# The message stage of a graph kernel: the last message product and the carry copies behind the third matrix product, and two pairs of PSUM banks that swap roles

## The reference

```
xs = concat(x[src, :8], x[dst, :8]); xv = the 3-vectors of both, 8 each
h  = sqrt(2) * relu(emb @ W1 / sqrt(10))                 # 16 hidden values per edge
w  = (h @ W2 / 4).reshape(E, 7, 16, 8)                   # seven weight blocks per edge
s_out, g_out = sums over xs, xv.y1 with w                # 8 and 8 values
v_out        = sums over xs*y1, xv, xv*y2 with w         # 8 vectors
out = concat(1.593*tanh(s_out), 1.593*tanh(g_out)[:, None] * v_out) * weight
layer = segment_sum(out, dst)
```

## Time and profile before

| what | value |
|---|---|
| median of 3 runs | 4437.76 us (4434.99 to 4440.44) |
| profiled execution: its own time | 4443.45 us |
| profiled execution: span from first to last instruction | 4441.7 us |
| DVE busy | 3024.5 us (68% of the span) |
| PE busy | 3333.9 us (75%) |
| POOL busy | 3235.5 us (73%) |
| ACT busy | 2187.2 us (49%) |
| mean granted TensorE clock | 0.953 |

### The profile page before, as it was taken

How to read it: one execution, slowest core, us unless ns; L and a number is a source line. 1 busy time by engine, 2 the same in 40 slices (tenths; PEclk the granted TensorE clock), 3 DMA queues, 4 the chain that set the end, 5 groups by cost and what they waited for, 6 DMA issues and landing times. The chain is left out here.

```text
span 4441.7 us, 66461 instructions
## 1 busy us (share of the span) xinstructions
PE 3333.9 (75%) x20487; PEld 2105.1 (47%) x20487; DVE 3024.5 (68%) x4871; ACT 2187.2 (49%) x4787; POOL 3235.5 (73%) x3260
## 2 busy tenths in 40 slices
PE   0005888888888888888888604999999999999940
PEld 0002333333333333323323203999999999999940
DVE  5525999999999999999999733344444544444432
ACT  3004555555555555555555311466666666666620
POOL 5777777777777777777774077777777777777756
PEclk9999999999999999999999856999999999999975
DMA  9311222222222222222222102133333333333311
GB/s 325 90 49 34 49 48 48 55 50 47 48 48 48 48 50 53 48 47 48 48 47 43 34 12 68 42 72 73 72 73 72 73 72 73 72 73 72 73 29 27
DMA packets 269592, 272.69 MB, mean 61 GB/s; under 512 B 182593, under 2 KB 237673, under 8 KB 266803
## 3 DMA queue, kind: packets, MB, share of 16 engines
q1 hardware_dynamic: 164150, 207.75, 17.0%
q0 software_dynamic: 104928, 60.74, 9.6%
q10 hardware_dynamic: 462, 3.60, 0.3%
HBM read 181.82 MB, written 90.02 MB: 61 GB/s over the span
## 5 line engine op out<-in xcount | busy, mean ns | idle before, releaser
L640 POOL DMA_INDIRECT edge<-xp_d,idx x1440 | 1447.3, 1005 | 439.1 <-issue 425.1
L900 DVE TENSOR_TENSOR prod<-G_ps,hid 128x1000 f32<-128x1000 f32 x1200 | 1400.4, 1195 | 125.8 <-PE G_ps L782 113.1
L1297 POOL DMA_INDIRECT x1e<-tab_d,idxb x1122 | 1105.4, 985 | 342.7 <-issue 336.4
L782 PE MATMUL G_ps<-FT,wst 32*128 32x500 f32 x4800 | 896.3, 633 | 356.8 <-DVE prod L900 350.0
L1346 PE MATMUL G_ps<-tb,hot 128*126 128x442 f32 (+1 forms) x3968 | 799.1, 358 | 0.9 <-DVE x1e L1371 0.8
L1346 PEld LDWEIGHTS G_ps<-tb,hot 128*126 128x126 f32 x3968 | 742.7, 187 | 38.4 <-DVE x1e L1371 2.0
L782 PEld LDWEIGHTS G_ps<-FT,wst 32*128 32x128 f32 x4800 | 246.3, 184 | 792.2 <-DVE prod L900 724.6
L811 PE MATMUL R_ps<-prod,red 128*32 128x500 f32 x4800 | 589.7, 594 | 0.0
L702 ACT ACTIVATE hid<-T_ps 128x500 f32<-128x500 f32 x400 | 233.8, 585 | 677.4 <-PE T_ps L802 677.1
L1346 PE MATMUL T_ps<-tb,hot 128*126 128x442 f32 x2000 | 416.4, 360 | 186.3 <-DVE one_d L1430 186.3
L1346 PEld LDWEIGHTS T_ps<-tb,hot 128*126 128x126 f32 x2000 | 376.6, 188 | 205.0 <-issue 186.4
(11 more groups left out here) (240 smaller groups left out, 4290.1 us busy)
## 6 DMA issues: line engine op xcount, KB each, us to landing
xd_d<-zeros SPq DMA_DIRECT2D x16, 1562.5 KB, 29.2
y_d<-ng SPq DMA_DIRECT2D x40, 595.0 KB
edge<-xp_d,idx POOLq DMA_INDIRECT x1440
xv<-xd_d SPq DMA_DIRECT2D x40, 560.0 KB
y_d<-zr SPq DMA_DIRECT2D x40, 560.0 KB
x1e<-tab_d,idxb POOLq DMA_INDIRECT x1122
edge<-sel_d SPq DMA_DIRECT2D x20, 750.0 KB
edge<-sel_d SPq DMA_DIRECT2D x20, 687.5 KB
```

The costliest lines, as they stand in the source:

```text
L640: nc.gpsimd.indirect_dma_start(out=edge_c[:, i, 8:8 + DIM], out_offset=None, in_=xp_d, in_offset=bass.IndirectOffsetOnAxis(col, 0)).then_i ...
L782: return Tn.matmul(G_ps[pair][:, a * 512:a * 512 + GW], wst[rows, r * 128:(r + 1) * 128], FT[k][rows, :], start=True, stop=True)
L900: V.tensor_tensor(prod[b][i][:, :].rearrange("p (a e) -> p a e", a=2), gv, hid[k][:, :].rearrange("p (a e) -> p a e", a=1).broadcast_to([1 ...
L1297: nc.gpsimd.indirect_dma_start(out=gx[b][:, c * T1:(c + 1) * T1], out_offset=None, in_=tab_d, in_offset=bass.IndirectOffsetOnAxis(idx[b][: ...
```

## The change

In the code of the message stage:

- `round1` is split. `round1a` (two products) is issued at the end of the group before, behind its `sum_round`s, and waits only for that group's first two products (`b_mul` >= 3n - 1). `round1b` (the other two) stands at the old place and waits for `b_mul` >= 3n as before. `b_G` is counted after each half.
- The bank pairs take turns: group n's first and third product read `G_ps[k]`, the second reads `G_ps[1 - k]`.
- On VectorE the second product has a wait of its own, for `round1b`.
- `post(2)` moves from between the second and third product of an odd group to the end of the even group before it, behind `post(0)`, `post(1)` and the scan.
- `carry_x` moves from gc 0 to the end of gc 9 of the chunk before; `carry_sums` moves, within gc 4, behind `post(1)`.

```diff
-                    def round1(n, k):
+                    def round1a(n, k):
                         pe.wait_ge(S("b_FT"), n + 1)
                         if some(n):
+                            pe.wait_ge(S("b_mul"), n * 3 - 1)
+                        product(k, 0, 0, k, 0)
+                        product(k, 0, 1, k, 1).then_inc(S("b_G"), 1)
+
+                    def round1b(n, k):
+                        if some(n):
                             pe.wait_ge(S("b_mul"), n * 3)
-                        product(k, 0, 0, 0, 0)
-                        product(k, 0, 1, 0, 1)
-                        product(k, 0, 2, 1, 1)
-                        product(k, 0, 3, 1, 0).then_inc(S("b_G"), 1)
+                        product(k, 0, 2, 1 - k, 1)
+                        product(k, 0, 3, 1 - k, 0).then_inc(S("b_G"), 1)
 
                     def round2(n, k):
                         pe.wait_ge(S("b_mul"), n * 3 + 1)
-                        product(k, 1, 0, 0, 0)
-                        product(k, 1, 1, 0, 1).then_inc(S("b_G2"), 1)
+                        product(k, 1, 0, k, 0)
+                        product(k, 1, 1, k, 1).then_inc(S("b_G2"), 1)
...
-                            round1(n, k)
+                            round1b(n, k)
...
+                            if not (last and g == G2 - 1):
+                                round1a(n + 1, 1 - k)
...
                         if i == 0:
                             dve.wait_ge(S("b_hid"), n + 1)
-                            dve.wait_ge(S("b_G"), n + 1)
+                            dve.wait_ge(S("b_G"), n * 2 + 1)
+                        if i == 1:
+                            dve.wait_ge(S("b_G"), n * 2 + 2)
...
-                        gv = G_ps[(0, 1, 0)[i]][:, :].rearrange("p (a e) -> p a e", a=2)[:, :, 0:GW]
+                        gv = G_ps[(k, 1 - k, k)[i]][:, :].rearrange("p (a e) -> p a e", a=2)[:, :, 0:GW]
...
-                            if k == 1 and not (first and g < 5):
-                                q = (g - 5) // 2
-                                post(2, t * RING + q, q % RING // PC, q % RING % PC, t if q >= 0 else t - 1)
-                            if gc == 0 and not (last and h == 1):
-                                carry_x(ch + 1, 1 - h)
-                            if gc == 4 and not (first and h == 0):
-                                carry_sums(ch - 1, 1 - h, t - 1 + h)
                             multiply(n, k, b, 2)
...
+                                if gc == GC - 1 and not last:
+                                    carry_x(ch + 2, h)
+                            else:
                                 q = (g - 4) // 2
+                                due = not (first and g < 4)
+                                if due:
+                                    for i in range(2):
+                                        post(i, t * RING + q, q % RING // PC, q % RING % PC, t if q >= 0 else t - 1)
+                                if scan:
+                                    scan()
+                                if gc == 4 and not (first and h == 0):
+                                    carry_sums(ch - 1, 1 - h, t - 1 + h)
+                                if due:
+                                    post(2, t * RING + q, q % RING // PC, q % RING % PC, t if q >= 0 else t - 1)
```

More of the change, by code:

```diff
@@ L845, in _ @@
                     transposes(1, 1, 0)
+                    round1a(0, 0)
                     turn(0, first=True)
@@ L974, in turn @@
                                     along(t * RING + q, q % RING)
-                            elif not (first and g < 4):
+                                if gc == GC - 1 and not last:
+                                    carry_x(ch + 2, h)
+                            else:
                                 q = (g - 4) // 2
[L977 to L980, removed]
+                                due = not (first and g < 4)
[8 more added lines that the diff above has]
+                                    post(2, t * RING + q, q % RING // PC, q % RING % PC, t if q >= 0 else t - 1)
                     for h in range(2):
@@ L993, in _ @@
                         along(p, p)
+                    carry_x(1, 1)
                     turn(0, first=True)
```

## The result

| what | before | after |
|---|---|---|
| median of 4 runs | 4439.10 us (4434.99 to 4441.09) | 4387.38 us (4385.00 to 4395.44) |
| ratio, 95% interval | | 0.9886 (0.9870 to 0.9901) |
| profiled execution: time, span | 4443.45, 4441.7 us | 4395.44, 4393.7 us |
| message stage, start of the first to start of the last product | 2150.1 us | 2099.4 us |
| one chunk, mean of 32 in the middle | 53.72 us | 52.57 us |

In the two traces, whose spans lie 48.0 us apart, the message stage is 50.8 us shorter, so the gain lies there and nowhere else. Medians and ratios are those of undisturbed executions; one of e6's four, which took 5387.23 us at a granted clock of 0.668, is left out.

What follows compares the result with a forecast made beforehand. VectorE's own order of work was taken to bound the message stage. Even groups, odd groups and gc 9 sum to 0.95 us per chunk, 38 us over 40 chunks; forecast median 4400 us, range 4389 to 4424.

Steps and rivals of the forecast that it cites:

- Odd groups: Groups losing `post(2)`: third product then held by `round2` alone, interval 5.37 to 5.22 us, 0.15 won each.
- gc 9: Chunk's last group into the next: first product no longer behind the third through `round1`, 0.30 us won a chunk.
- Even groups: Groups gaining `post(2)` behind the scan: it replaces the wait for TensorE, interval 5.43 to 5.42 us, 0.01 won each.
- the 0.14: Even groups: time in us from TensorE's end to the first product's start, kept unchanged in the new sum.
- Both chains stand at 5.41: Even groups: VectorE's and TensorE's new chains equally long at 5.41 us, so every delay shows.
- Stage ends: Both ends of the message stage: untouched by the change, no gain counted there.
- A: TensorE, odd groups: split halves run one after the other, +6 us, 4444, no change; chance 0.08.
- B: TensorE: halves in turn and each split costs its entry as well, slower at 4474 us; chance 0.06.
- C: Even groups: scan and `post(2)` pay full length and a gap, 30 us back, 4430, half of it 4415; chance 0.08.
- D: POOL: scans stretch gathers until they bind, 22 us come back, 4422; chance 0.06.
- The estimate was 54: POOL: room in us between last gather's end and last `turned` after the change, 91 before it.
- estimate of 10.48 a piece: POOL: a piece's eight gathers at 1.31 us each take 10.48 us, undisturbed 10.0; not binding.

Runs made afterwards that it cites:

- e6: The kernel after, with `turned` moved between second and third product in odd groups other than gc 9; 4355.99 us, ratio 0.9817.
- e3: The kernel before, with VectorE's order of the kernel after (`post(2)` and carry copies moved), `round1` whole; 4410.72 us, ratio 0.9935.
- e8: e3 with VectorE's two waits ahead of the first product swapped; 4394.21 us, ratio 0.9902.
- e1: The kernel before, with only VectorE's two waits ahead of the first product swapped; 4416.16 us, ratio 0.9952.
- e2: The kernel after, with VectorE's order of the kernel before (`post(2)` and carry copies back), `round1` still split; 4401.18 us, ratio 0.9917.
- e4: The kernel after, but the first product of odd groups waits for both halves of `round1`; 4393.36 us, ratio 0.9898.
- e5: The kernel after, with `carry_x` back between second and third product in gc 0; 4385.33 us, ratio 0.9883.
- e7: e6 with `carry_x` in gc 0 and `post(0)` in gc 2, 4, 6, 8 ahead of the third product; 4382.26 us, ratio 0.9874.
- e9: e6 with `carry_x` in gc 0 and the scan in gc 2, 6, 8 ahead of the third product; 4349.15 us, ratio 0.9805.

## Why the prediction came out as it did

**Odd groups: right.** 5.22 was forecast, 5.23 came. The third product starts some 2.4 behind the first (3.60 less one product of 1.20) and `turned` follows it. e3 shows it without the split.

**gc 9: right in size, wrong in part of its reason.** 0.30 forecast, 0.31 measured. Its reason was that it "exists only because `round1a` no longer waits for the third product". e3, with `round1` whole, has 4.92 and wins 0.15; e8 has 4.85 and wins 0.22, 0.07 of it the form of the wait. The split (with the banks) is behind the last 0.09. So the 0.30 was VectorE's chain read rightly, but most of it didn't need the split.

**Even groups: the step that failed.** "Ready at 1307.46, plus the 0.14 from PE's end to the product's start now: 1307.60, interval 5.41." The 0.14 was carried over as if it were the way from TensorE to VectorE. It belonged to one form of waiting. In after the same way is 0.05, in e1, where the form alone is changed, 0.07, and gc 4, where TensorE's chain ends last, shows the term bare:

- before: 1.25 (first product to `round2`) + 2.92 (to `round1`) + 1.12 + 0.14 = 5.43;
- after: 1.25 + 2.92 (1291.36 to 1294.28) + 1.11 + 0.05 = 5.33.

So TensorE's bound was mis-sized by 0.08, and the edit that changed the wait's form, the new threshold of the first product's wait, is one that the prediction did not price at all. VectorE's own chain, forecast at 5.41, came to 5.39 to 5.40 (`post(2)` to the next product 0.32) and is what ends last in even groups but gc 4. "Both chains stand at 5.41" was therefore not so: one had 0.07 to spare.

e1, e3 and e8 show that 0.07 of gc 4's 0.10 is the wait's form, and that the other even groups' step from 5.43 (e3) to 5.40 (e8) is nothing else. On top of the moves the form is worth 42.5 - 27.7 = 15 us, about what the forecast fell short by; the split and the banks, which the prediction took for the cause of the even groups' 0.01 and gc 9's 0.30, are worth 7 to 9 us in all. The last 0.03 (5.36 in e1 and e8, 5.33 in e2 and after) comes with the split. e4 gives 5.39 where both halves are awaited, which is more than the unsplit round of e8 costs; why two counted halves cost 0.03 more than one round isn't settled.

**Stage ends: wrong.** "Stage ends are untouched." The first 20 groups took 106.3 us instead of 112.2, of which 2.3 is the regular gain of two chunks. Nearly all of the rest lies in the first three: 17.8 us instead of 21.5. While the first pieces have no sums to post, VectorE has little to do behind its third product. In before it waits 1.56 for `round1`, and its third product waits 1.03 for `round2`:

```profile
379.40 2.31 DVE L900 TENSOR_TENSOR prod<-G_ps,hid 128x1000 f32<-128x1000 f32 x2 [1.56 <-PE G_ps L782]
...
382.74 1.20 DVE L900 TENSOR_TENSOR prod<-G_ps,hid 128x1000 f32<-128x1000 f32 x1 [1.03 <-PE G_ps L782]
```

and after, where the first two groups stand 4.27 apart instead of 5.91:

```profile
374.08 3.61 DVE L909 TENSOR_TENSOR prod<-G_ps,hid 128x1000 f32<-128x1000 f32 x3 [7.88 <-PE G_ps L782]
...
378.35 3.58 DVE L909 TENSOR_TENSOR prod<-G_ps,hid 128x1000 f32<-128x1000 f32 x3
```

Two things are mixed there. One is the split: the first two groups stand 4.27 to 5.20 apart in every kernel that has it and 5.36 to 6.86 in every one that hasn't. The other is TensorE's granted clock. From 377 to 394 us it was 0.51 in before and 0.80 in after, and second passes on line 782 that last 0.58 at 2.4 GHz last 1.04 at 1.2. Line 782 has 36 passes of over 0.9 us in before, none behind 394, and 16 in after:

```profile
377.00:394.00 17.00, 14.74 (x56) 4.76 (x60) 10.30 (x12) 4.77 (x10) 13.02 (x14) 0.51 0.08 13
```

```profile
377.00:394.00 17.00, 14.71 (x70) 4.61 (x66) 12.82 (x14) 5.35 (x11) 13.03 (x14) 0.80 0.10 14
```

The second trace of after has 36 such passes too (though its clock column shows 1.00), and its first three groups took 20.1. So of the 3.7 won there, about 1.4 stands beside a start with equally long passes; the other 2.3 goes with the higher clock of the first trace. The last 20 groups took 100.7 instead of 104.2 in both traces of after, 1.2 more than two chunks' gain. There the odd groups of the last chunk have no scan, and TensorE ends last as in gc 9: 5.15 in before, 4.94 in e8, 4.57 to 4.62 in after.

**The rivals.** A (the halves one after the other) fell: both halves into an odd group are one row of 1.12, where two rounds in turn would need 2.2, and e2 gains instead of losing. The Trainium skill, "TensorE: Matmul & The Clock Gate", section "The mechanism", has matmuls start and end strictly in program order; taken for whole products of two passes it speaks for A, and the row of 1.12 speaks against that reading. B needed A and fell with it. C (the even group pays for `post(2)`) fell as a loss: 5.39 to 5.40, below its old time. Yet it had the right place: `post(2)` takes back 0.07 of each gain of 0.10 there, as e2 beside after shows. D (POOL takes over) fell: no `turned` waits for a gather. The last `turned` starts at 2444.19, 38 us behind the last gather's end at 2406.2. The estimate was 54: up to there the stage won 49 us instead of 38, and the gathers ended 5 later than in before.

## What to carry to other kernels

When a measured way from one engine's end to another's start goes into a sum, look at how that wait is made (of two plain waits here, the one written first was carried by the instruction), and whether the edit leaves the same wait on the instruction: here the order of two waits was worth 22 us of 4438 by itself. Price two edits that open and fill the same hole together, not one by one: 37 and 28 us alone made 50. And what goes into a hole must have its inputs by then: a scan did, `post(0)`, which needs ScalarE, did not.

## What the runs showed of the hardware

**A late wait that isn't carried by the instruction cost 0.07 us.** Where two waits stand ahead of the first product, before and e1 have one of them as a sequencer instruction. With the late one there, the product started 0.14 behind TensorE's end. e1 swaps the two and nothing else: 0.07. In after, where the first two of four products are awaited, it is 0.05.

**Gathers fall into step with the scans.** The mean distance of two gathers' starts on line 640, first to last over 1439, and the chunk divided by it:

| | distance, us | gathers a chunk |
|---|---|---|
| before | 1.310 | 41.0 |
| after | 1.314 | 40.0 |
| e1, e2, e3 | 1.300, 1.291, 1.294 | 41.0 |
| e4 | 1.285 | 41.0 |
| e5, e6 | 1.311, 1.294 | 40.0 |
| e7 | 1.283 | 40.9 |
| e8 | 1.316 | 40.1 |
| e9 | 1.287 | 40.0 |

The line's rows of e4 and of e8 (columns as in the earlier trace rows):

```profile
L640 POOL DMA_INDIRECT edge<-xp_d,idx x1440: 940/944/1542, 511.4 to 2361.1; - x180
```

```profile
L640 POOL DMA_INDIRECT edge<-xp_d,idx x1440: 940/944/1553, 514.6 to 2408.2; - x180
```

A chunk uses 40 gathers. e4 and e8 have nearly the same chunk (52.71 and 52.72), and their gathers go at different paces, each close to a whole number to a chunk (e7, with 40 in some chunks and 41 in most, is the exception); no gap ahead of a gather is longer there than the 0.3 that it always has. The trace of after shows how a scan sets the phase. From 560 to 2300 us 265 gathers start while a scan runs, and all of them end 0.75 to 0.77 behind that scan's end, wherever in it they started. Two examples are the scan at 1283.81 (0.84 long, shown above) with POOL's gather at 1283.89, and this scan with the gather at 1289.46. From the scan's end to the gather's it is 1285.40 - 1284.65 = 0.75 and 1290.46 - 1289.70 = 0.76:

```profile
1288.87 0.83 DVE L880 TENSOR_TENSOR_SCAN ds<-kp,xt 125x328 f32<-125x328 f32 x1
```

```profile
1283.89 1.51 POOL L640 DMA_INDIRECT edge<-xp_d,idx  x1 [0.30 <-issue]
...
1289.46 1.00 POOL L640 DMA_INDIRECT edge<-xp_d,idx  x1 [0.31 <-issue]
```

So their pace is set by the scans' rhythm, not by a length of their own, and the prediction's estimate of 10.48 a piece, taken as fixed, was wrong in kind: after has 8 x 1.314 = 10.51, which is its chunk over 5. Why it is once 40 and once 41 stays open.

**A scan can be the one that is held.** The longest `sums` scan is 853 ns in before and 900 in e4, where 33 of them from 560 to 2300 us, one a chunk, are over 870 (after has a single one, of 896 ns at 458.4 us). e4's row (least, median, longest; first and last start):

```profile
L952 DVE TENSOR_TENSOR_SCAN Z<-kpp,O x160: 816/833/900, 457.4 to 2491.4; 125x328 f32<-125x328 f32 x160
```

That is the scan of gc 5 at 1300.79 above, 0.88 long in an interval of 5.29 instead of 5.23. A gather starts within 0.01 of it (1300.79 in POOL's timeline), and so it is for all 33: the gather starts 0.00 to 0.03 behind the scan's start and takes its undisturbed 0.94. The Trainium skill, "SBUF — State Buffer", section "Who interferes with whom", gives the shared ports to whichever of the two issues first. The trace agrees where the scan is in front: the gather then ends behind it. It doesn't agree where a gather is: in after 132 gathers run when a scan starts, none takes over 0.96 and none of the scans over 0.84. The held scan's price here is 0.07, not a gather's length.
